# First attention put into one program with feed-forward and second attention, and the general path tested at the end

## What is computed

```python
# layer 0
q, k = x @ Wq + bq, x @ Wk + bk
attn = softmax(q @ k.T / sqrt(32))                 # per graph and head, 256 x 256
out  = sum(((adj == r) * attn) @ (x @ Wv[r] + bv[r]) for r in range(4))
x    = layernorm(x + out @ Wo + bo, g1, beta1)
x    = layernorm(x + gelu(x @ W1 + b1) @ W2 + b2, g2, beta2)   # FF = 1024
# layer 1
e    = leaky(q @ k.T, 0.2)
attn = softmax(where(adj > 0, e, -9e15))
h    = layernorm(attn @ v, g1, b1)
out  = layernorm(concat([h, x]) @ Wffn.T, g2, b2) + x
```

## Time and profile before

| | us |
|---|---|
| median of 3 runs (3158.16 to 3162.86) | 3160.52 |
| the profiled execution, its own time | 3157.04 |
| its span, first to last instruction | 3155.3 |
| PE busy in the span | 3019.6 (96%) |
| DVE / ACT / POOL busy | 2482.2 / 1999.8 / 1672.7 |
| mean granted clock of TensorE | 0.987 |

### The profile page before, as it was taken

The page is one execution under the profiler, slowest core; times in us unless marked ns, Lnnn a source line. Parts: engine busy times, 40 slices in busy tenths (PEclk is TensorE's granted clock), DMA queues, the critical chain, the costliest instruction groups (busy, mean ns, idle before and its releaser), DMA issues.

```text
span 3155.3 us, 75174 instructions
## 1 busy us (share of the span) xinstructions
PE 3019.6 (96%) x27909; PEld 2049.3 (65%) x27909; DVE 2482.2 (79%) x6757; ACT 1999.8 (63%) x3695; POOL 1672.7 (53%) x1511
## 2 busy tenths in 40 slices
PE   6999999999999976999999998999999999999996
PEld 4666666666666644666666676777777777777773
DVE  5888888888888864666666667888888888888883
ACT  4666656666666644666666656777777777777774
POOL 2555555555554542344444435666666666666665
PEclk9999999999999998999999999999999999999998
DMA  5444444544454423222222224444444444444441
GB/s 163 138 135 140 135 140 131 144 129 145 130 144 131 142 62 92 76 77 78 81 68 81 77 86 142 136 136 147 137 142 140 138 142 135 136 147 137 142 129 41
DMA packets 358327, 382.45 MB, mean 121 GB/s; under 512 B 99264, under 2 KB 266816, under 8 KB 357952
## 3 DMA queue, kind: packets, MB, share of 16 engines
q1 hardware_dynamic: 356800, 376.03, 40.3%
q10 hardware_dynamic: 1152, 1.52, 0.2%
HBM read 242.16 MB, written 118.49 MB: 114 GB/s over the span
## 4 chain that ended last, share of the span: by engine, by line
PE 54%; DVE 2%; DMA 2%; issue 1%; ACT 1%; SPq 1%; POOL 0%; POOLq 0%; DVEq 0%; ACTq 0%
PE bank_heads L2267 4%; PE bank_pair L2146 4%; PE bank_pair L2535 3%; PE bank_pair L2537 3%; PE bank_pair L2536 3%; PE bank_score L2171 3%; PE bank_pair L2149 3%; PE bank_pair L2160 3%; PE bank_proj L2131 2%; PE bank_proj L2133 2%; PE bank_proj L2132 2%; PE bank_back L2131 2%; PE bank_heads L2535 2%; PE bank_heads L2536 2%; PE bank_heads L2537 2%; PE bank_sums L2536 2%
## 5 line engine op out<-in xcount | busy, mean ns | idle before, releaser
L1865 ACT ACTIVATE f_gh<-bank_pair 128x512 f32<-128x512 f32 x512 | 304.3, 594 | 247.3 <-PE bank_pair L2149 247.2
L2488 DVE TENSOR_TENSOR f_gl<-f_act,f_gh 128x512 f16<-128x512 f32 x256 | 281.9, 1101 | 227.1 <-ACT f_act L2416 227.1
L2075 DVE CUSTOM_DVE_ANT_0 b_junk<-bank_score,b_mask 128x256 bf16<-128x256 f32 x1024 | 390.6, 419 | 42.1 <-issue 41.8
L1409 DVE TENSOR_TENSOR a_linked<-a_prob,a_mask 128x1024 f32<-128x1024 f32 x256 | 354.0, 1383 | 3.9 <-ACT a_prob L1206 3.9
L1968 POOL TENSOR_TENSOR f_xb<-f_gh 128x512 f32<-128x512 f32 x256 | 335.6, 1311 | 36.0 <-ACT f_gh L1865 35.7
L2411 ACT ACTIVATE f_gh<-bank_pair,s_f_b 128x512 f16<-128x512 f32 x256 | 175.7, 686 | 252.7 <-PE bank_pair L2537 252.6
L1952 POOL TENSOR_TENSOR b_nw_root<-b_nw_var,b_minus_halves 128x2 f32<-128x2 f32 x128 | 113.0, 883 | 406.8 <-DVE b_nw_neg_mean L2016 406.8
L1206 ACT ACTIVATE a_prob<-a_score_t 128x1024 f32<-128x1024 f32 x256 | 259.5, 1014 | 109.0 <-PE a_score_t L1489 103.0
L1402 DVE TENSOR_REDUCE a_neg_max<-a_score 128x4 f32<-128x1024 f32 x256 | 307.5, 1201 | 2.7 <-PE a_score L1502 2.6
L1871 ACT ACTIVATE bank_pair<-bank_pair 128x512 f32<-128x512 f32 x512 | 305.4, 596 | 0.0
L1447 DVE SCALAR_TENSOR_TENSOR a_qk<-a_proj,a_vcol,a_qk 128x256 f16<-128x256 f32 x256 | 112.1, 480 | 136.6 <-ACT a_qk L1217 136.6
(11 more groups left out here) (275 smaller groups left out, 9748.3 us busy)
## 6 DMA issues: line engine op xcount, KB each, us to landing
a_stack<-qk_scratch SPq DMA_DIRECT2D x384, 128.0 KB, 3.0
qk_scratch<-a_qk SPq DMA_DIRECT2D x64, 512.0 KB, 2.9
qk_scratch<-b_qk SPq DMA_DIRECT2D x64, 512.0 KB, 2.9
first_rows<-qk_scratch SPq DMA_DIRECT2D x192, 128.0 KB, 3.0
f_gl<-qk_scratch SPq DMA_DIRECT2D x192, 128.0 KB, 2.8
a_x_sb<-x_t SPq DMA_DIRECT2D x64, 256.0 KB, 3.3
a_adj_sb<-adj_t SPq DMA_DIRECT2D x64, 256.0 KB, 3.1
a_res<-x_nodes SPq DMA_DIRECT2D x64, 256.0 KB, 3.4
```

The costliest lines, as they stand in the source:

```text
L1409: nc.vector.tensor_tensor(linked[:, k], prob[:, k], mask[:, be[1] % 2].unsqueeze(1).to_broadcast([P, 2, NT * N]), ALU.mult).then_inc(link_ ...
L1865: nc.scalar.activation(prob[:, he], score_t[s].rearrange("p t n -> p (t n)"), ACT.Exp, scale=ALPHA).then_inc(exp_done, 1)
L2075: last = nc.vector.tensor_tensor_reduce(junk[:, s, it], score[s][:, it], mask[:, i, it], -1.0, 3e38, ALU.add, ALU.min, neg_max[:, i, col:c ...
L2488: nc.vector.tensor_tensor(gl[:, bu[1] % 2, f], act32[:, f % 2], gh[:, bu[1] % 2, f], ALU.subtract).then_inc(low_done, 1)
```

## The change

All three stages stand in one program, `all_stages`. Feed-forward's slot 0 falls on first attention's slot START = 524; second attention joins 31 feed-forward steps after that, as before. Within a slot each engine first does what first attention has there, then feed-forward, then second attention. First attention uses PSUM banks of the others (its scores those of `up`, its transposed scores those of `down`), and feed-forward's buffers lie over first attention's in SBUF. So feed-forward's first uses of a buffer wait for counts of first attention (`wait_first`). The splits of W1 and W2 are cut in four each and stand in steps 8 to 11 and 18 to 21; W2's load is in step 16. The check of the edges is in first attention's slots 560 to 562. The general path is tested after all stages; behind it a second copy of all stages but the first stands under the same test.

```diff
+    FPARTS = 8
+    W2_STEP = 16
+    ffn_part = {(W2_STEP + 2 if n >= FPARTS // 2 else W2_STEP - FPARTS) + n % (FPARTS // 2): n for n in range(FPARTS)}
...
-                    if number(t) in (B + 1, B + 4) and h == 7:
-                        part = number(t) > B + 1
-                        act.wait_ge(ffn_loaded, 32 if part else 16)
-                        nc.scalar.activation((w2 if part else w1)[:, 0].rearrange("p c n -> p (c n)"), stage_f, ACT.Copy).then_inc(ffn_high, 1)
+                    if h == 7 and number(t) in ffn_part:
+                        n = ffn_part[number(t)]
...
+                        nc.scalar.activation((w2 if second else w1)[:, 0].rearrange("p c n -> p (c n)")[:, cols], stage_f[:, cols], ACT.Copy).then_inc(ffn_high, 1)
...
+                    if number(t) == B + STEPS_TAIL and h == 0:
+                        dve.wait_ge(edges_seen, B)
...
-        score = psum("score", [P, 2, NT, N])
-        score_t = psum("score_t", [P, 2, NT, N])
+        score = banks["pairs"][:].rearrange("p (e t n) -> p e t n", e=2, t=NT)
+        score_t = banks["down"][:].rearrange("p (e t n) -> p e t n", e=2, t=NT)
...
+                        if number(bl) == 0:
+                            wait_first(sp, "w2_split")
+                        if first:
+                            for k in range(2):
+                                sp.wait_ge(first["rows"][k], (number(bl) + 1) * 16)
                         sp.dma_start(x_sb[:, i].rearrange("p (g t) n -> p g (t n)", g=G), pair_rows(x_in, bl)).then_inc(x_loaded[i], 16)
...
                 if h == 4 and number(t) == 2:
+                    wait_first(sp, "values")
...
+                        if number(bu) == 0 and f == 0:
+                            wait_first(act, "scores_t_61", "qk_stored0", "qk_stored1", "v_ready")
                         nc.scalar.activation(gh[:, i, f], up[s][:], ACT.Gelu, bias=b1[:, f:f + 1]).then_inc(gelu_high, 1)
...
+                        if number(bx) == 0:
+                            wait_first(act, "proj_done")
...
+                        if number(bx) == 0:
+                            wait_first(pool, "proj_done", "qk_stored0", "qk_stored1")
...
+                        if number(bu) < 2 and f == 0:
+                            wait_first(dve, "scores_t_62" if number(bu) else "values_61")
...
+                        if number(bu) == 0 and f == 0:
+                            wait_first(pe, "max_done")
...
+                        if number(bd) == 0 and f == 0:
+                            wait_first(pe, "exp_done")
...
+    START = 524
+    JOIN = 31 * H
...
+            for g in range(BEGIN + JOIN + H * second["steps"]):
+                if zero_slot and g < H * zero["steps"]:
+                    zero_slot((g // H // U, g // H % U), g % H)
+                if g == BEGIN:
+                    first_slot = first[name](eng)
+                n = g - BEGIN
+                if 0 <= n < H * first["steps"]:
+                    first_slot((n // H // U, n // H % U), n % H)
...
+                if n >= JOIN:
+                    second_slot(((n - JOIN) // H // U, (n - JOIN) // H % U), n % H)
...
-        attention_first(nc, x_t, mid1, adj_t, w0, scr, scr_m, shared, wf, other_edges)
+        joint = (mid1, mid2, out, adj, adj_t, scr1, scr_m, shared, w1, wf, other_edges)
+        all_stages(nc, *joint, first_in=(x_t, mid1, adj_t, w0, scr, scr_m, shared, wf, other_edges))
         attention_layer(nc, 0, x_t, mid1, adj_t, w0, scr, consts, other_edges, general=True)
...
-        feed_forward_and_second(nc, mid1, mid2, out, adj, adj_t, scr1, scr_m, shared, w1, late)
+        all_stages(nc, *joint)
```

More of the change, by code:

```diff
@@ L1197, in _, with slot @@
             act.dma_start(shared["f_b1"][:], wf["f_b1"]).then_inc(consts_in, 16)
-            def step(t):
-                for h in range(H):
+            def slot(t, h):
+                if True:
                     if due_pair := pair_due(t, h, "exp"):
@@ L1654, in sem, with again @@
             return sems[-1]
+        past = {}
+        def again(name, n=None):
+            signal, past[name] = before.get(name, (None, 0))
+            if signal is None:
+                signal = [sem(f"{name}{i}") for i in range(n)] if n else sem(name)
+            return signal
         def over(buffer, first, shape, dt):
@@ L2124, in slot @@
                         norm_stats(bg, 1, y[:, bg[1] % 2], y_ready)
-            return slot
+            return slot, first_constants
         def tensor(pe):
```

396 lines of the change are left out of this document (215 added, 181 removed).

## The result

Changed kernel, 6 runs: median 3145.26 us (3139.71 to 3150.05). Kernel before, 6 runs in the same comparison: 3159.40 us (3154.54 to 3162.86). The ratio is 0.9951, 95% interval 0.9939 to 0.9963: faster by 0.49%; the two medians lie 14.1 us apart. The forecast was 24.4 us less, 3134. Direction and range held; 10 us of the gain are missing, and the rest of the text looks for them.

A forecast was written before the change was run, and what follows sets the result against it. The prediction took TensorE as the bound, with gains only where it stands still. Joint -40.2, end +14.8 and splits +1.0 made -24.4 us: 3132.6 from the profiled 3157.0, 3136.1 from the median, forecast 3134 between; range 3116 to 3152.

The forecast's parts named there:

- What bounds the kernel: Whole kernel: TensorE (PE) is the bound, so the change can win only where PE stands still.
- The splits: W1 and W2 pieces in steady feed-forward steps: +1 us, ends 0 and 6.
- the joint: From slot 524 to feed-forward's step 3, plus trailing attention work: 75.8 us in place of 116.0, 40.2 saved.
- Slots 524 to 531: First attention's slots beside feed-forward's step 0: 16.5 us, ends 14.8 and 20, with POOL's 2.34 us on the path.
- Slots 532 to 539: The next eight slots, where `exp` and Gelu take turns: ACT bounds, not PE; 27 us, ends 20.1 and 33.
- Slots 540 to 547: The next eight slots: 30.5 us, ends 27.4 and 34, with about 3 us waiting for the last `exp`.
- trailing work: First attention's last PE work behind slot 547: 1.8 us, between matmuls that leave PE no gap.
- The end: Behind the last store: two tests between barriers with nothing to hide them, +14.8 us, ends 11 and 18.
- Switches cost more than their load: Rival, slots 532 to 540: each of nine table switches costs another 1.28 us, 11.5 more, about 3145; chance 0.12.
- The joint hides all: Rival, the joint: ACT runs ahead, only PE's work counts, 51.9 us saved instead of 40.2, 3122; chance 0.15.
- The clock: Rival, slots 532 to 547: PE, held up by ACT, gets the lower clock, +37.5 us, 3171; chance 0.06.
- No overlap: Rival: feed-forward waits until first attention's last result, only barrier and test leave the middle, 3162 us; chance 0.07.

The follow-up runs named there:

- e11: The kernel before, with only W1 and W2 split in eight pieces in steps 8 to 11 and 18 to 21: median 3150.7 us, ratio 0.9987 to before.
- e2: The changed kernel with GpSimd's `f_xb` of feed-forward's first three pairs moved behind `a_hl`: median 3137.1 us, ratio 0.9939 to the kernel before.
- e3: The changed kernel with Identity for Gelu in feed-forward's first pair and an eighth of the second: median 3135.5 us, ratio 0.9932 to the kernel before.
- e8: The changed kernel with all work on loaded x of feed-forward's first three pairs two slots later: median 3135.6 us, ratio 0.9933 to the kernel before.
- e10: The changed kernel with START = 540 and the first three pairs' work on x two slots later: median 3136.0 us, ratio 0.9936 to the kernel before.
- e1: The changed kernel without the general path, the second copy of all stages and both end tests: median 3131.1 us, ratio 0.9921 to the kernel before.

## Why the forecast was right, and by how much it was off

**What bounds the kernel: right.** PE is busy as before in the steady stretches, and a feed-forward step is still 20.85 us (1268 to 1468: PE busy throughout).

**The splits: within the ends.** Forecast +1 in the steady steps (0 to 6) and 0.7 back in slots 524 to 531; e11 shows 0.9 there, and 6.9 us less drain against 4 to 5 less time, so some 2 or 3 for the pieces, with an uncertainty larger than itself. The other 6 us of the drain are no gain on top: the changed kernel has no drain, and they are part of the 116.0 us that the joint replaced. What I had not seen is how much of that drain was the splits' own.

**Slots 524 to 531: the step that failed most, 20.6 in place of 16.5.** The larger part is a term that the sum did not have: "a clock at or near 1.00 there". Behind the 4.17 us wait TensorE ran at the lower level for about 6.5 us (1137.4 to 1143.9), which costs about 3.2 us. The waits grew from 3.1 us in the kernel before to 5.7, by 2.6 where 1.6 had been forecast. "POOL's 2.34 us stay on the path" took `f_xb` at its duration from a place where the other engines stood idle; beside VectorE it took 3.33, and it began only at 1132.13, since ahead of it `a_z_out` took 2.15 us beside an `a_linked`, so that `a_hl` was done 3.0 us later than in the earlier trace rows (1137.56 against 1134.53). The work of 10.7 us was priced too low as well: the earlier trace rows has 11.60 for it.

**Slots 532 to 539: size nearly right (29.5 for 27), reason half right.** ScalarE's sum was 25.0 us against the 26.2 forecast. But it was busy 85%, not over 90%, and of the longest wait there, 3.64 us, GpSimd's hold on VectorE made 2.15, which the prediction did not have; e2 takes them off without touching ScalarE. The other 1.49 are VectorE's wait for a Gelu. Behind the wait for `a_y` came 3.5 us at half clock. The switches that the prediction did have are real (e3).

**Slots 540 to 547 (34.2 for 30.5) and trailing work (3.3 for 1.8).** The `exp` wait before the first `down` was 1.44 us in place of about 3; another 3.40 for an `a_linked` under `f_xb` came, 2.8 us of half clock behind it, and at the end `out` waited 1.55 us for an `a_hl` behind the `f_xb` of 3.34 us at 1218.28. That is the fourth pair's `f_xb`, which e2 and e8 left in its place, and there the wait stayed (1.56 and 1.55 us). "Between matmuls that leave PE no gap" did not hold for that last one.

**The end: right, 12.9 for 14.8**, in 6.5 and 6.1 us, and PE's jump did not follow the code that is skipped: over the general path it took 3.42 us in the kernel before, 4.34 in the changed one and 4.44 in e10, and over the second copy of all stages 3.80.

**The rivals.** "Switches cost more than their load" had given 3145, the number that came out, for a reason that did not: the loads are 1.28 us with nothing around them, and without them the joint gains 7.2 us at most, not 23. With the rule of the Trainium skill, page "ScalarE: Activation LUTs", section "What ACT_TABLE_LOAD costs", the forecast would have hit the time and missed the cause; no row here has the drain of which it speaks. "The joint hides all" failed at the waits. "The clock" was right in kind: it cost about 5 to 6 us, a sixth or seventh of its 37.5. "No overlap" did not happen.

**The missing 11.7 us of the joint, added up.** The forecast's 75.8 us were 60.0 of work and 15.8 of waits. TensorE's listed waits are 19.3: 3.5 us more. Half clock took 12.7 us (summed in windows of 0.5 us: 1137.4 to 1143.9, 1170.9 to 1174.4, 1188.4 to 1191.4), which costs about 6, and the forecast had nothing for it; by the column "rest" against e10 it is 5.0. The last 2 to 3 us are work priced too low: e10 needs 102.3 us beside its waits, and the prediction's prices with the 39.1 us from step 3 on make 99.1. So waits were the smaller error, and the clock that falls behind them the larger one. How much of both is `f_xb`: 5.1 to 5.4 us of waits by e2; what it adds through the clock can't be told from two profiles, since half clock differs by as much between e1 and the changed kernel.

## What to carry to other kernels

When two stages are laid over each other, list for each moved GpSimd instruction which VectorE instruction with two inputs in SBUF will start beneath it, and who waits for that one. Here three `f_xb` of about 3 us cost TensorE 1.5, 2.15 and 2.15 us of waiting, and no busy share shows it. Place such work right behind the instruction that TensorE waits for; that alone took 5 us of waits, the later start 2.7, both 7.7. List likewise which instruction of one stage stands, in each queue, behind one that waits for the other stage. A price read from an idle stretch was too low in a full one (`f_xb` 2.34 against 3.33). And a sum that has waits of 3 to 4 us for TensorE should have a term for the clock behind them: here it was larger than the error in the waits.
